# The spread G row of layers 2 and 3: ACT copies it from SBUF to PSUM, where TensorE made five transposes

## The chip, the cores and the metric

One core of a Trainium2 chip runs the whole kernel in one launch. The metric is the device time of the execution in microseconds (us); less is better. The engines are TensorE (PE; its weight loads are listed as PEld), VectorE (DVE), ScalarE (ACT), GpSimd (POOL) and SyncE (SP, which here only starts DMAs).

## The reference

A graph network with 3125 nodes of 128 features and 103125 directed edges (among them one self loop per node, to which each layer adds one more). `x = x + L0(relu(layernorm(x)))`, where L0 is two graph-attention layers with a relu between them; then `x = x + L1(relu(layernorm(x)))`, where L1 is one. Each attention layer does, for its own weights:

```python
h = x @ W
s = h @ a_src
d = h @ a_dst
e = leaky_relu(s[src] + d[dst], 0.2)
m = segment_max(e, dst)
ex = exp(e - m[dst])
out = segment_sum((ex / z[dst])[:, None] * h[src], dst)   # z = segment_sum(ex, dst)
```

The edge features are not used for the result.

## The kernel before, in words

**Dense attention over counts.** The edge list is first turned into a table C of counts (how many edges go from node i to node j, one byte each), which stays in SBUF. The three attention layers then work on dense tiles. The exponential of a leaky relu of a sum falls apart into factors of source and destination: for a source tile and a destination row it is, up to factors that are applied elsewhere, the larger of a number per source (`r_src`) and a number per destination, the G row (`g_row`), times the count.

**Chunks and tiles.** The 3125 nodes are 25 tiles (T) of 125 (P). A layer goes through its destinations in 5 chunks (NC) of 625 columns (CD, five tiles of 125), and in each chunk through the 25 source tiles s. Chunks are numbered q = 0 to 14 through all three layers (Q = 15), c = q % 5 within a layer, and a chunk that opens layer 2 or 3 (q = 5, 10) is called a turn.

**One source tile, two ways.** The weights of source tile s are max(G row, r_src) times the counts, 125 x 625, in one of nine buffers (`slot`). Most even tiles are made by VectorE in one instruction (`product`, line 1023), which reads the G row, spread over all partitions, from PSUM at column 1024 (ROWU). The tiles in `POOL_OF` (the odd ones from 3 on; in layers 2 and 3 also 6, 12 and 18, in layer 3 also 0; in the turns 20 and 22) are made by ACT and POOL: ACT takes the maximum in two instructions (`row_maximum`, lines 1428 and 1434), reading a second copy of the spread G row in SBUF (`ga`, one buffer for odd and one for even chunks), and POOL multiplies with the counts (line 662). TensorE then multiplies each finished tile with the features of its sources (`products`, line 1679; the last two tiles of a chunk in `last_products`, line 1687). A float32 matmul is two records in the trace, a transpose one.

**Where the two copies of the G row come from.** `g_row` holds the numbers with the destinations over partitions. For PSUM, TensorE spreads a column with a transpose of a broadcast, five per chunk (`fast_rows`, line 1663), at source tile `rows_at` (22, in a turn 23) of the chunk before; it waits until VectorE's last product and joined top of that chunk are done. For SBUF, SP writes `g_row` to DRAM once per layer part (`write_lines`, line 469) and loads 625 numbers, broadcast to all partitions, one chunk ahead (`ga_load`, line 478); ACT's first row maximum of a chunk waits for that load (`ga_loaded`).

**The order on each engine** is written out by hand, by chunk and source tile. Where a chunk ends:

- VectorE makes the product of tile 24, then five steps of the running maxima of the *next* chunk (`next_top`, lines 947 and 945; the steps 0 to 4 need no G row), then waits for `rows_ready` and makes the product of tile 0 (where POOL has tile 0, in chunks 11 to 14, it only waits).
- ACT makes its row maxima six source tiles ahead (`PASS_AHEAD`). At tile 24 it makes that of tile 5 of the next chunk, which waits until TensorE is through tile 21 and so has freed the buffer. Then it moves the sums of the finished chunk out of PSUM (`move_sums`, lines 1402 and 1405), at tile 0 of the next.
- TensorE, after the transposes, does the last products and those of tiles 0 and 1, then transposes the joined maxima (`top_transpose`, line 1649), which VectorE reduces (line 957). In a turn that transpose stands at the end of the chunk before.
- The middle of a chunk holds the work on the sums of the chunk before: normalisation (statistics on VectorE, scalars on POOL, line 1374 on ACT), transposes (1702) and new features (1732 or 1735) on TensorE, and moves of them on ACT (1345, 1366).

```python
dve.wait_ge(F.rows_ready, q + 1)
v.scalar_tensor_tensor(slot[s]..., tiles(ROWU), r_src[L % 2][:, s:s + 1], C5[:, c, s, :]..., ALU.max, ALU.mult)
```

Of the kernel before, what the change touches and what calls it, by code (L numbers as in the profile page):

```python
# [7 lines left out]
def gat_stack_kernel(nc, x, edges, apart, W1, a_src1, a_dst1, b1, W2, a_src2, a_dst2, b2,  # L8
# [3 lines left out]
    ALU, ACT, AX = mybir.AluOpType, mybir.ActivationFunctionType, mybir.AxisListType  # L12
# [6 lines left out]
    P = 125  # L19
    T = N // P  # L20
# [14 lines left out]
    CT = 5  # L35
# [28 lines left out]
    with ctx:  # L64
# [351 lines left out]
        def rows_at(q):  # L416
            return 23 if turn(q) else 22
# [4 lines left out]
        def prod_no(q, s):  # L422
            return q * T + s - pool_no(q, s)
# [836 lines left out]
        def _(act):  # L1260
# [151 lines left out]
            def row_maximum(q, s):  # L1412
# [16 lines left out]
                if q < NC:  # L1429
# [4 lines left out]
                a_.activation(A, A, ACT.Identity, bias=r_src[L % 2][:, s:s + 1],  # L1434
                              scale=r_src[L % 2][:, s:s + 1]).then_inc(rowmax_ok, 1)

            def scale_features(s):
                a_.activation(hB3[:, s, :], hA[:, s, :], ACT.Copy, scale=e_src[0][:, s:s + 1]).then_inc(h_scaled, 1)

            def chunk(q):  # L1440
                L, c = q // NC, q % NC
                for s in range(T):
                    if q == 0 and s + FIRST < T:
                        scale_features(s + FIRST)
                    if q:
                        if s == 0:
                            move_sums(q - 1, True)
                        if s == post_at(q).kappa:
                            factors(q - 1)
                        after_sums(F, q - 1, post_at(q), s)  # L1450
                    if c == NC - 1 and L < LAYERS - 1:
                        if s == 10:
                            act.wait_ge(sig_ready, L + 2)
                            exps_dst(L + 1, 0, EARLY_TILES)
                            exps_src(L + 1, 0, EARLY_TILES)
                        if s == T - 1:
                            act.wait_ge(F.new_sb, q)
                            exps_src(L + 1, EARLY_TILES, LATE)
                    if turn(q):
                        if s == post_at(q).act[2]:  # L1460
                            act.wait_ge(F.new_sb, q)
                            exps_src(L, LATE, T)
                        if s == 22:
                            exps_dst(L, EARLY_TILES, T)
                    for i in (q, q + 1):
                        for p in POOL_OF[i] if i < Q else ():
                            if pass_at(i, p) == q * T + s:
                                row_maximum(i, p)

            act.wait_ge(half_out[0], T + 1)  # L1470
            act.wait_ge(half_out[1], T + 1)
# [79 lines left out]
        def _(pe):  # L1551
# [100 lines left out]
            def fast_rows(q):  # L1652
                L, c = q // NC, q % NC
                if c == 0:
                    pe.wait_ge(g_done, LINES[L, 0])
                elif L and c == EARLY_TILES // CT:
                    pe.wait_ge(g_done, LINES[L, EARLY_TILES])
                if q:
                    pe.wait_ge(prod_done, prod_no(q, 0))
                for t in range(CT):  # L1660
                    if t == CT - 1 and q:
                        pe.wait_ge(F.top_done, q * (T + 1))
                    last = tr(ps[0:P, ROWU + 128 * t:ROWU + 128 * t + P],  # L1663
                              g_row[L % 2][:, c * CT + t:c * CT + t + 1].broadcast_to([P, P]), ident[0:P, 0:P])
                last.then_inc(F.rows_ready, 1)
# [83 lines left out]
            def chunk(q):  # L1749
                L, c = q // NC, q % NC  # L1750
                for s in range(T):
# [12 lines left out]
                    if q:  # L1764
# [4 lines left out]
                                pe.wait_ge(ga_ready, 1)  # L1769
                            top_transpose(F, q - 1)  # L1770
                        after_sums(F, q - 1, post_at(q), s)
                    if s == rows_at(q) and q < Q - 1:
                        fast_rows(q + 1)
                    if s == T - 1 and c == NC - 1:
                        if L < LAYERS - 1:
# [111 lines left out]
```

## Time and profile before

| what | value |
|---|---|
| runs of the kernel, median of 3 | 758.86 us (758.7 to 760.88) |
| the profiled execution, its own time | 762.35 us |
| its span, first to last instruction | 760.5 us |
| TensorE busy | 654.9 us (86%) |
| VectorE busy | 695.5 us (91%) |
| ACT busy | 506.4 us (67%) |
| POOL busy | 372.1 us (49%) |
| mean granted clock of TensorE | 0.933 of full speed |

Up to about 228 us the counts are made; then come the fifteen chunks, five per layer. The times of the trace are microseconds from the start of the span. A busy share is a mean over all stages, and an engine that is busy for nearly all of a chunk is a candidate for its bound. A number in brackets behind a timeline row is how long the engine stood before the instruction, and for whom; a row without one had no wait that the profile records. The span of an instruction can overlap the next one's by some 0.1 us, as engines are pipelined.

### The profile page before, as it was taken

The numbers are of one execution on the slowest core, as the hardware profiler recorded it, in microseconds if no ns is written. First come the engines' busy times: TensorE is split into PE (matmuls) and PEld (weight loads), VectorE is DVE, ScalarE is ACT, GpSimd is POOL, SyncE is SP. The second block draws the span as 40 slices with busy tenths as digits, with TensorE's granted clock in tenths as the row PEclk, the third lists the DMA queues.
The fourth block names the chain that finished last, engine by engine and source line by source line (L and its number), as shares of the span: only waits on it lengthen the run. The fifth ranks groups of instructions, "written<-read, shape, count | busy, mean of one in ns | idle before, by whom it ended". The sixth has DMA issues, their size and how long they took to land.

```text
span 760.5 us, 14385 instructions
## 1 busy us (share of the span) xinstructions
PE 654.9 (86%) x5581; PEld 637.2 (84%) x5581; DVE 695.5 (91%) x903; ACT 506.4 (67%) x739; POOL 372.1 (49%) x344
## 2 busy tenths in 40 slices
PE   2429999999858999999998989999979989998994
PEld 2428888889758999999998989998969888998984
DVE  3799999999959999999998899899998989999994
ACT  1205454545539987878776777878776698697880
POOL 5030000000323673645494567667587776795873
PEclk9959899899857999999999989999999999999998
DMA  3310000000003232222133232222033223323211
GB/s 81 97 43 1 1 1 2 1 1 1 1 8 59 74 104 79 82 78 74 31 74 118 72 75 100 75 82 75 27 67 95 72 66 84 108 92 118 79 55 39
DMA packets 50145, 45.39 MB, mean 60 GB/s; under 512 B 13458, under 2 KB 47995, under 8 KB 50070
## 3 DMA queue, kind: packets, MB, share of 16 engines
q1 hardware_dynamic: 49270, 43.14, 19.8%
q0 software_dynamic: 800, 1.26, 0.6%
q8 instruction: 46, 0.75, 0.4%
q14 instruction: 29, 0.24, 0.1%
HBM read 31.34 MB, written 13.05 MB: 58 GB/s over the span
## 4 chain that ended last, share of the span: by engine, by line
PE 29%; DVE 21%; issue 8%; DMA 5%; ACT 3%; POOL 3%; DVEq 0%; SPq 0%; POOLq 0%
PE ps L1679 23%; DVE ps L945 10%; DVE scratch L1023 5%; DVE ps L947 2%; DMA g_lines<-g_row 1%; DMA gathered<-ext_lines 1%; ACT scratch L1428 1%; POOL scratch L662 1%; PE ps L1687 1%; PE ps L1732 1%; DVE mu L957 1%; DMA gathered<-g_lines 1%; PE ps L1710 1%; ACT scratch L1434 1%; ACT scratch L1374 1%
## 5 line engine op out<-in xcount | busy, mean ns | idle before, releaser
L1679 PE MATMUL ps<-hB,scratch 125*125 125x129 f32 x3450 | 408.9, 277 | 29.6 <-DVE scratch L1023 22.5
L1679 PEld LDWEIGHTS ps<-hB,scratch 125*125 125x125 f32 x3450 | 394.5, 190 | 39.1 <-DVE scratch L1023 29.4
L662 POOL TENSOR_TENSOR scratch<-scratch 125x625 f32<-125x625 f32 x197 | 262.0, 1338 | 155.6 <-ACT scratch L1434 142.7
L945 DVE SCALAR_TENSOR_TENSOR ps<-C,a_unit,ps 125x625 f32<-125x625 uint8 x330 | 277.0, 863 | 2.1
L1428 ACT ACTIVATE scratch<-gathered,r_inv 125x625 f32<-125x625 f32 x197 | 159.1, 808 | 34.9 <-PE ps L1679 28.3
L1434 ACT ACTIVATE scratch<-scratch,r_src 125x625 f32<-125x625 f32 x197 | 178.4, 905 | 4.7
L1023 DVE SCALAR_TENSOR_TENSOR scratch<-ps,r_src,C 125x625 f32<-125x625 f32 x178 | 152.7, 858 | 10.8 <-PE ps L1663 10.2
L1610 PE MATMUL ps<-scratch 128*128 128x125 bf16 x1250 | 148.3, 296 | 15.5 <-DVE scratch L856 12.0
L1610 PEld LDWEIGHTS ps<-scratch 128*128 128x128 bf16 x1250 | 143.2, 121 | 19.2 <-DVE scratch L856 12.7
L1304 ACT ACTIVATE C<-ps 125x1750 uint8<-125x1750 f32 (+3 forms) x50 | 74.3, 1488 | 107.6 <-PE ps L1610 107.6
L856 DVE TENSOR_TENSOR scratch<-key_col,hB 128x6500 bf16<-128x6500 bf16 (+3 forms) x26 | 92.8, 3569 | 0.0
L856 DVE TENSOR_TENSOR scratch<-key_lo,hB 128x6656 bf16<-128x6656 bf16 (+3 forms) x26 | 88.0, 3383 | 4.2 <-PE ps L1610 4.2
L712 POOL TENSOR_TENSOR xr<-xr,b2r 125x3200 f32<-125x3200 f32 x1 | 7.3, 7338 | 151.3 <-ACT hA L1292 151.3
L1432 ACT ACTIVATE scratch<-C 125x625 bf16<-125x625 uint8 x55 | 39.3, 715 | 0.0
L1687 PE MATMUL ps<-hB,scratch 125*125 125x129 f32 x300 | 35.6, 273 | 0.0
L1687 PEld LDWEIGHTS ps<-hB,scratch 125*125 125x125 f32 x300 | 34.2, 187 | 0.1
L947 DVE TENSOR_SCALAR ps<-C,a_unit 125x625 f32<-125x625 uint8 x30 | 25.9, 863 | 3.6 <-ACT C L1304 2.6
L672 POOL TENSOR_TENSOR scratch<-scratch,rz 125x640 f32<-125x640 f32 x14 | 17.6, 1254 | 7.6 <-DVE rz L1000 7.4
L1366 ACT ACTIVATE hA<-ps 125x384 f32<-125x384 f32 (+1 forms) x20 | 8.3, 442 | 17.3 <-PE ps L1732 12.1
L1589 PE MATMUL ps<-covered,ones_f 125*125 125x1 f32 x2 | 0.6, 358 | 20.2 <-DVE covered L837 20.2
L1589 PEld LDWEIGHTS ps<-covered,ones_f 125*125 125x125 f32 x2 | 0.5, 308 | 20.5 <-DVE covered L837 20.5
L1402 ACT ACTIVATE scratch<-ps 125x387 f32<-125x387 f32 x15 | 7.3, 489 | 15.4 <-PE ps L1687 15.3
(161 smaller groups left out, 430.6 us busy)
## 6 DMA issues: line engine op xcount, KB each, us to landing
scratch<-counts_bf SPq DMA_DIRECT2D x142, 152.6 KB
counts_bf<-scratch SPq DMA_DIRECT2D x73, 152.6 KB
gathered<-g_lines SPq DMA_DIRECT2D x14, 305.2 KB
xr<-in_x SPq DMA_DIRECT2D x1, 1562.5 KB
out<-xr SPq DMA_DIRECT2D x5, 312.5 KB
edge_sb<-in_edges SPq DMA_DIRECT2D x1, 805.7 KB
gathered<-ext_lines SPq DMA_DIRECT2D x5, 122.1 KB
w<-in_W SPq DMA_DIRECT2D x2, 128.0 KB
```

Source lines behind the costliest of these rows:

```text
L662: g.tensor_tensor(slot[s], slot[s], wide[r % WIDE], ALU.mult).then_inc(pool_done, 1)
L856: last = v.tensor_tensor(hot[:, g0:g1, :, :], keys.unsqueeze(2).broadcast_to([128, g1 - g0, m, LANES]), iota_t[:, 0:m, :].unsqueeze(1).bro ...
L945: v.scalar_tensor_tensor(dest, counts, unit[:, s:s + 1], top, ALU.min, ALU.max).then_inc(S.top_done, 1)
L947: v.tensor_scalar(dest, counts, unit[:, s:s + 1], None, ALU.min).then_inc(S.top_done, 1)
L1023: v.scalar_tensor_tensor(slot[s].rearrange("p (t n) -> p t n", n=P), tiles(ROWU), r_src[L % 2][:, s:s + 1], C5[:, c, s, :].rearrange("p (t ...
L1304: a_.activation(C5[:, c, :, rows].rearrange("p t (w q) -> p t w q", q=WQ), tiles(at_, w1_ - w0).rearrange("p w (t q) -> p t w q", q=WQ), A ...
L1428: a_.activation(A, ga[q % 2], ACT.Relu, bias=-1.0, scale=r_inv[L % 2][:, s:s + 1]).then_inc(over_done, 1)
L1432: a_.activation(wide[r % WIDE], C5[:, c, s, :], ACT.Copy).then_inc(cast_act, 1)
L1434: a_.activation(A, A, ACT.Identity, bias=r_src[L % 2][:, s:s + 1], scale=r_src[L % 2][:, s:s + 1]).then_inc(rowmax_ok, 1)
L1610: last = mm(ps[0:128, o:o + WC], hot_lo[i][:, at_g, :, lane], hot_col[i][:, at_g, :, lane], start=(k == 0), stop=(k == KC - 1))
L1679: last = mm(ps[0:P, acc_at(t):acc_at(t) + HW], A[:, P * t:P * (t + 1)], feat, start=opens and t in (0, 3), stop=closes, skip_group_check=True)
L1687: last = mm(ps[0:P, acc_at(t):acc_at(t) + HW], slot[s][:, P * t:P * (t + 1)], hB3[:, s, :], start=False, stop=s == T - 1, skip_group_check ...
```

## The change

TensorE's `fast_rows` is called for chunks 0 to 4 only. For chunks 5 to 14 a new function of ACT, `copied_rows`, copies the spread G row from `ga` in SBUF to ROWU in PSUM in one ACTIVATE of 125 x 625. It stands at the end of source tile 24 of the chunk before, behind that tile's row maxima, and waits for the load of `ga`, for VectorE's last product and for the joined top. It raises the same semaphore that VectorE waits for.

```diff
--- before.py
+++ after.py
@@ -1434,6 +1434,12 @@
                 a_.activation(A, A, ACT.Identity, bias=r_src[L % 2][:, s:s + 1],
                               scale=r_src[L % 2][:, s:s + 1]).then_inc(rowmax_ok, 1)
 
+            def copied_rows(q):
+                act.wait_ge(ga_loaded, 16 * q)
+                act.wait_ge(prod_done, prod_no(q, 0))
+                act.wait_ge(F.top_done, q * (T + 1))
+                a_.activation(tiles(ROWU), ga[q % 2].rearrange("p (t n) -> p t n", n=P), ACT.Copy).then_inc(F.rows_ready, 1)
+
             def scale_features(s):
                 a_.activation(hB3[:, s, :], hA[:, s, :], ACT.Copy, scale=e_src[0][:, s:s + 1]).then_inc(h_scaled, 1)
 
@@ -1466,6 +1472,8 @@
                         for p in POOL_OF[i] if i < Q else ():
                             if pass_at(i, p) == q * T + s:
                                 row_maximum(i, p)
+                    if s == T - 1 and NC - 1 <= q < Q - 1:
+                        copied_rows(q + 1)
 
             act.wait_ge(half_out[0], T + 1)
             act.wait_ge(half_out[1], T + 1)
@@ -1653,8 +1661,6 @@
                 L, c = q // NC, q % NC
                 if c == 0:
                     pe.wait_ge(g_done, LINES[L, 0])
-                elif L and c == EARLY_TILES // CT:
-                    pe.wait_ge(g_done, LINES[L, EARLY_TILES])
                 if q:
                     pe.wait_ge(prod_done, prod_no(q, 0))
                 for t in range(CT):
@@ -1769,7 +1775,7 @@
                                 pe.wait_ge(ga_ready, 1)
                             top_transpose(F, q - 1)
                         after_sums(F, q - 1, post_at(q), s)
-                    if s == rows_at(q) and q < Q - 1:
+                    if s == rows_at(q) and q < NC - 1:
                         fast_rows(q + 1)
                     if s == T - 1 and c == NC - 1:
                         if L < LAYERS - 1:
```

`prod_no(q, 0)` is the number of products that VectorE has made when chunk q begins, and `q * (T + 1)` that of the steps and joins of the maxima.

## Rows read from the trace of the kernel before

**Rows 1.** total of the waits (who <- for whom: us, times, longest)

```profile
DVE scratch L1023 <- PE ps L1663: 10.2, 6, 2.9
```

**Rows 2.** windows, chunk 8 (length; PE, PEld, DVE, ACT, POOL busy; PEclk, DMA, GB/s)

```profile
511.64:544.94 33.30, 31.11 (x278) 30.52 (x277) 32.58 (x55) 27.65 (x42) 23.12 (x21) 1.00 0.21 64
```

**Rows 3.** timeline, boundary into chunk 8 (start, us, engine, instruction, [idle before])

```profile
511.59 0.91 ACT L1434 ACTIVATE scratch<-scratch,r_src 125x625 f32<-125x625 f32 x1
511.64 0.71 PE L1663 MATMUL ps<-ident,g_row 125*125 125x125 f32 x5
512.46 0.87 DVE L1023 SCALAR_TENSOR_TENSOR scratch<-ps,r_src,C 125x625 f32<-125x625 f32 x1
517.43 0.81 DVE L957 TENSOR_REDUCE mu<-ps 125x5 f32<-125x625 f32 x1 [0.22 <-PE ps L1649]
```

**Rows 4.** timeline, boundary into chunk 5

```profile
403.66 0.71 PE L1663 MATMUL ps<-ident,g_row 125*125 125x125 f32 x5
404.51 0.87 DVE L1023 SCALAR_TENSOR_TENSOR scratch<-ps,r_src,C 125x625 f32<-125x625 f32 x1 [1.53 <-PE ps L1663]
406.41 0.71 PE L1649 MATMUL ps<-ident,scratch 125*125 125x125 f32 x5
406.83 0.91 ACT L1434 ACTIVATE scratch<-scratch,r_src 125x625 f32<-125x625 f32 x1
413.87 4.86 PE L1679 MATMUL ps<-hB,scratch 125*125 125x129 f32 x40 [0.94 <-DVE scratch L1023]
```

**Rows 5.** groups by line, ACT, 625 columns (count; busy us, mean ns; idle before)

```profile
L1432 ACT ACTIVATE scratch<-C 125x625 bf16<-125x625 uint8 x55 | 39.3, 715 | 0.0
L1345 ACT ACTIVATE scratch<-ps 128x625 f32<-128x625 f32 x10 | 6.8, 678 | 4.1 <-PE ps L1702 4.1
L1434 ACT ACTIVATE scratch<-scratch,r_src 125x625 f32<-125x625 f32 x197 | 178.4, 905 | 4.7
```

**Rows 6.** timeline, boundaries into chunks 6, 10, 11, 12 and 13

```profile
441.33 0.91 ACT L1434 ACTIVATE scratch<-scratch,r_src 125x625 f32<-125x625 f32 x1
441.93 0.86 DVE L1023 SCALAR_TENSOR_TENSOR scratch<-ps,r_src,C 125x625 f32<-125x625 f32 x1
...
584.50 0.87 DVE L1023 SCALAR_TENSOR_TENSOR scratch<-ps,r_src,C 125x625 f32<-125x625 f32 x1 [2.88 <-PE ps L1663]
584.85 0.91 ACT L1434 ACTIVATE scratch<-scratch,r_src 125x625 f32<-125x625 f32 x1
...
620.66 0.87 DVE L947 TENSOR_SCALAR ps<-C,a_unit 125x625 f32<-125x625 uint8 x1
621.72 0.91 ACT L1434 ACTIVATE scratch<-scratch,r_src 125x625 f32<-125x625 f32 x1
622.54 0.47 ACT L1402 ACTIVATE scratch<-ps 125x387 f32<-125x387 f32 x1
...
653.16 0.91 ACT L1434 ACTIVATE scratch<-scratch,r_src 125x625 f32<-125x625 f32 x1
653.96 0.87 DVE L947 TENSOR_SCALAR ps<-C,a_unit 125x625 f32<-125x625 uint8 x1 [1.06 <-PE ps L1663]
658.99 0.81 DVE L957 TENSOR_REDUCE mu<-ps 125x5 f32<-125x625 f32 x1 [0.29 <-PE ps L1649]
...
683.52 0.91 ACT L1434 ACTIVATE scratch<-scratch,r_src 125x625 f32<-125x625 f32 x1
686.75 0.87 DVE L947 TENSOR_SCALAR ps<-C,a_unit 125x625 f32<-125x625 uint8 x1
```

**Rows 7.** windows after two long stops of TensorE

```profile
451.50:455.50 4.00, 4.00 (x18) 4.00 (x19) 3.51 (x8) 2.42 (x4) 2.21 (x2) 0.50 0.29 69
570.60:573.00 2.40, 2.39 (x12) 2.40 (x13) 2.40 (x4) 2.37 (x4) 2.40 (x3) 0.50 0.22 14
```

**Rows 8.** timeline, TensorE after the same two stops

```profile
451.50 14.21 PE L1679 MATMUL ps<-hB,scratch 125*125 125x129 f32 x100 [2.99 <-DVE scratch L1023]
...
570.61 1.30 PE L1702 MATMUL ps<-ident,scratch 125*128 125x125 f32 x5 [2.68 <-ACT scratch L1374]
```

## The prediction

> **What bounds the kernel now.** I read the total of the waits first, then the busy time of one chunk, then the instructions on both sides of each boundary between two chunks, since that is the only place the change touches. The change concerns ten boundaries, those into chunks 5 to 14.
>
> The reader is to see three things. First, VectorE seldom waits for the five transposes: six times, 10.2 us in the whole run [rows 1]. Second, inside layer 2 VectorE is the bound: from the transposes of one chunk to those of the next are 33.30 us, of which VectorE is busy for 32.58 and TensorE for 31.11 [rows 2]. Third, the boundary into chunk 8 is exactly tight [rows 3]. TensorE begins the five transposes at 511.64 and ends them at 512.35; VectorE, with the five tiles of work that it does ahead just behind it, starts the first product of the chunk at 512.46 without a recorded wait. ACT, at the same moment, is not early: its last row maximum of the chunk starts at 511.59 and lasts 0.91 us. The new copy stands behind that instruction.
>
> **The change, part by part.** *Removed:* five transposes at ten boundaries. Five of them last 0.71 us to the end of the last one [rows 3, 4], but TensorE goes on to the next instruction before that: 278 records in 31.11 us [rows 2] is 0.11 us from one to the next, so it gets back 5 x 0.11 = 0.55 us per boundary, 5.5 us in all. I put this at nothing: behind the transposes TensorE does its last products and then needs the first product of the new chunk, which VectorE makes later than now. What hides it is VectorE's lateness; were TensorE the bound, the whole 5.5 us would be a gain (a rival below). The dropped wait of TensorE on g_done costs and gives nothing, since the DMA that ACT waits for already stands behind the same exponentials.
>
> *Added on ACT:* ten copies of 125x625 float32. The trace has no ACT instruction that reads SBUF and writes PSUM at this size. The nearest row is the plain Copy of L1432, SBUF to SBUF, the same 625 columns with no scale or bias from memory: 715 ns [rows 5]. Bounds are the plain Copy out of PSUM, 678 ns, and the Identity with a scale and a bias from memory, 905 ns [rows 5]. I take 0.715, for the lack of such operands. Page "ScalarE: Activation LUTs" of the Trainium skill (the tips under "Step-by-step: what each stage is for") says that PSUM is the lower-latency destination for ACT; no row here has that direction, and if writing PSUM saved what reading it does, 0.04 us a copy, the sum below would be 0.3 us smaller.
>
> The copy starts 0.82 us after the start of the L1434 before it (the spacing to the next instruction on ACT, 621.72 to 622.54 [rows 6], a little under its 0.91 duration), ends 0.72 later, and VectorE takes some 0.04 to start: **1.58 us after the start of that L1434**. That sum is now applied to each boundary.
>
> *Waits added for ACT:* for the row's DMA, which the first row maximum of the same chunk has already waited for; for the last product and the joined top of the old chunk, which VectorE made before it went ahead. All are past. *Behind the copy on ACT* stand the moves of the sums (L1402): in layer 2's steady chunks they wait for TensorE anyway. SP's and POOL's queues get nothing and lose nothing; POOL's products wait for ACT's row maxima, which move 0.7 us where ACT is dense. The copy writes the same columns of PSUM, so nothing else is moved.
>
> *Boundary into 5* [rows 4]: ACT is held by the round trip of the row through DRAM, its last L1434 starts at 406.83, rows now come at 408.41, and VectorE, which started at 404.51, loses **3.90**. TensorE waits 0.94 for VectorE at 413.87 already, so the loss reaches it, and from there TensorE is dense to the end of the chunk.
>
> *Into 6* [rows 6]: 441.33 + 1.58 = 442.91 against 441.93: **0.98**.
>
> *Into 8* [rows 3] *and 7* (the same pattern 33.3 us earlier): 511.59 + 1.58 = 513.17 against 512.46, 0.71. Of it 0.22 vanishes, because VectorE's reduction at 517.43 waits 0.22 for TensorE's transposes of the tops, which come no later than now: the 0.55 given back pays for the later first product. **0.49** twice. *Into 9*, the same pattern 33.3 us later, but small reductions stand where that wait was: **0.71**.
>
> *Into 10* [rows 6]: 584.85 + 1.58 = 586.43 against 584.50: **1.93**.
>
> *Into 11* [rows 6]: ACT is dense, its L1434 starts at 621.72; rows come at 623.30 where VectorE went on at 620.66: 2.64 late. From there to the next boundary VectorE has no wait. *Into 12*: it would arrive at 652.90 (653.96 less its wait of 1.06), with the delay 655.54, later than the copy (653.16 + 1.58 = 654.74), and 1.58 later than the 653.96 of now; the reduction at 658.99 had waited 0.29. Together **1.29** for both boundaries.
>
> *Into 13* [rows 6] *and 14* (the same pattern): copy ready at 683.52 + 1.58 = 685.10, VectorE wants it at 686.75: **0**, with 1.6 us to spare; here the first tile belongs to POOL, so VectorE needs the row later.
>
> Sum of delays: 3.90 + 0.98 + 0.49 + 0.49 + 0.71 + 1.93 + 1.29 = **9.8 us**. By the ends of the copy's price (678 and 905 ns) over seven binding boundaries it is 9.5 to 11.1.
>
> *TensorE's clock.* Where TensorE stood for 2.99 us (before 451.50) or 2.68 us (before 570.61) the granted clock was 0.50 afterwards, the 1.2 GHz level; after 0.94 us (413.87) the work ran at full speed [rows 4, 7, 8]. At half clock 18 records took 4.00 us in one window and 12 took 2.40 in the other; at 0.11 each they need 2.0 and 1.3, so such a fall costs at least 1.1 us and, as the first lasted longer than its window, up to 3.0 (100 records in 14.21 us [rows 8], 11.2 at that pace). Into chunk 5 TensorE will have finished the tops' transposes at about 406.5 and wait for the first product, done 0.87 after 408.41, at 409.28: a stop of 2.8 us, between the two that brought a fall, and more short stops follow it (the third product comes 3.9 late too). Part of the slow stretch lies under those stops. I take **1.5 us** for it, bounds 0 and 3.0, paid in full because TensorE is dense afterwards.
>
> Total 9.8 + 1.5 = **11.3 us**. The profiled execution took 762.35 us with a span of 760.5, so 1.85 lie around the span; it would become 773.7. The median of the runs is 758.86, 3.5 under the profiled one; the difference is carried over: **770.2 us**.
>
> **The rivals.**
>
> *A. The clock keeps full speed at chunk 5.* For: the stop is worked out to a few tenths of a microsecond, and the rows leave open what a stop between 0.94 and 2.68 us does; if the copy or the products come a little sooner it is such a one. Then 758.9 + 9.8 = 768.7.
>
> *B. More falls of the clock.* In chunk 11 TensorE waits for the moved sums, which start 0.72 after the 622.54 of now [rows 6] while TensorE is there 0.55 sooner, and again for products that VectorE makes 2.64 late. With 3.0 at chunk 5 and 1.5 here: 758.9 + 9.8 + 4.5 = 773.2. Against: in chunk 11 TensorE later waits for POOL, which would swallow most of it.
>
> *C. The delays are absorbed.* VectorE's lateness in the steady chunks may be taken up by TensorE's 0.55 and by the shared slack, so that only the boundaries where ACT is held by a DMA (5 and 10) count: 3.9 + 1.9 = 5.8, 764.7. If those are eaten too, 761. Against: VectorE is busy 32.58 of 33.30 us and has nowhere to catch up.
>
> *D. Faster: TensorE is the bound.* Place: the products behind the removed transposes. If each 0.55 us is on the path, the kernel takes 758.9 - 5.5 = 753.4. It decides from the point where ACT's copy is done before TensorE would have been: ACT's last L1434 would have to start some 0.8 us earlier than it does [rows 3]. For: TensorE is busy 31.11 us of the 33.30 [rows 2]. Against: ACT is late at every boundary up to 12 [rows 3, 4, 6].
>
> *E. The change does not relieve TensorE in profile terms* (transposes still there): not possible for chunks 5 to 14, as the call is taken out; no chance is given.
>
> **How the numbers follow.** Forecast (with one fall of the clock, and sizes within a microsecond or two) 0.50; A 0.24; B 0.08; C 0.12, of which 0.05 ends within 0.3%; D 0.05; the rest, 0.01, anything. A difference of 0.3% (2.3 us) is about what a measurement of this kernel can tell from none. Faster 0.05; same 0.06; slower 0.89. The range goes from C's 764.7 to B's 773.2, widened a little on each side for the copy's price: 764.3 to 774.0; outside are D, the end of C and the far side of B, together under 2 in 10.
>
> **What would show each step.** VectorE's wait for the row is then for the ACT copy: about 6 us or less into chunk 5 (1.53 now plus 3.9), under 1 us into chunk 8, over 2 us into 11, none into 13. The copy lasts 0.68 to 0.80 us. The stretch from the boundary into 8 to that into 9 grows from 33.30 to some 34 us; that from 13 to 14 stays as it is. The granted clock reads 0.5 for a few microseconds near 410 to 420. TensorE's idle time for VectorE's products grows by more than 5 us. The prediction is wrong if ACT's last row maximum comes earlier because TensorE ran ahead, if the copy takes over 1 us, or if layers 2 and 3 as a whole grow by less than 5 us.

## The result, and the profile after

| | before | after |
|---|---|---|
| median of 4 runs each | 759.36 us (758.7 to 760.88) | 772.26 us (769.86 to 774.13) |
| ratio | | 1.0165, 95% interval 1.0132 to 1.0199 |
| profiled execution, its span | 762.35, 760.5 | 769.86, 768.0 |
| TensorE, VectorE, ACT busy | 654.9, 695.5, 506.4 | 652.3, 695.8, 512.0 |
| mean granted clock | 0.933 | 0.933 |

The kernel became slower by 1.65%, 12.9 us between the medians. The predicted 770.2 us lies 2.1 us under the measured median, which is inside the range of 764.3 to 774.0. The two profiled executions differ by 7.5 us only, because that of before is slower than all four runs and that of after the fastest of its four; so times are compared by the runs, and the traces are used for places.

Lines behind the new function have moved down by six to eight in the kernel after: L1663 is L1669 there, L1679 is L1685, L1649 is L1657 and L1687 is L1693. `copied_rows` is L1441.

The total of the waits (who waited for whom: us in total, times, longest), first one row of the kernel before, then three of the kernel after, of which the first answers to [rows 1]:

```profile
PE ps L1679 <- DVE scratch L1023: 22.5, 25, 3.0
...
DVE scratch L1023 <- ACT ps L1441: 14.4, 6, 5.8
DVE ps L947 <- ACT ps L1441: 2.5, 1, 2.5
PE ps L1685 <- DVE scratch L1023: 35.3, 38, 3.0
```

VectorE waits for ACT's copy in seven of the ten places, for 16.9 us. In the kernel before it waited for the transposes into the same ten chunks four times, for 7.7 us: 1.53, 2.27 and 2.88 for the product and 1.06 for L947 [rows 3, 4, 6]. The 10.2 us of [rows 1] leave the last one out and hold 3.5 us of layer 1, which the change does not touch. VectorE's busy time did not change. TensorE had less to do and stood 12.8 us longer for VectorE's products.

The copy itself, by its line (duration in ns, least, median, most):

```profile
L1441 ACT ACTIVATE ps<-gathered x10: 672/673/675, 407.4 to 723.8; 125x625 f32<-125x625 f32 x10
```

Timeline of the kernel after at the boundary into chunk 9, the steady pattern, which answers to [rows 3]: ACT, then VectorE.

```profile
513.23 0.91 ACT L1434 ACTIVATE scratch<-scratch,r_src 125x625 f32<-125x625 f32 x1
514.04 0.67 ACT L1441 ACTIVATE ps<-gathered 125x625 f32<-125x625 f32 x1
514.82 0.87 DVE L1023 SCALAR_TENSOR_TENSOR scratch<-ps,r_src,C 125x625 f32<-125x625 f32 x1 [0.68 <-ACT ps L1441]
```

This boundary is put beside the boundary into 8 of before, since the pattern repeats. The copy starts 0.81 us after the start of the L1434 and VectorE 0.11 after the copy's end: 1.59 us after the start of the L1434, where the prediction had 1.58. The wait of 0.68 answers to the predicted 0.71.

Timelines of the kernel after, VectorE's first instruction that needs the row, into chunks 5, 6, 10, 11 and 13, which answer to [rows 4, 6]:

```profile
408.21 0.87 DVE L1023 SCALAR_TENSOR_TENSOR scratch<-ps,r_src,C 125x625 f32<-125x625 f32 x1 [5.63 <-ACT ps L1441]
...
445.50 0.87 DVE L1023 SCALAR_TENSOR_TENSOR scratch<-ps,r_src,C 125x625 f32<-125x625 f32 x1 [0.90 <-ACT ps L1441]
...
591.60 0.87 DVE L1023 SCALAR_TENSOR_TENSOR scratch<-ps,r_src,C 125x625 f32<-125x625 f32 x1 [5.80 <-ACT ps L1441]
...
630.35 0.87 DVE L947 TENSOR_SCALAR ps<-C,a_unit 125x625 f32<-125x625 uint8 x1 [2.50 <-ACT ps L1441]
...
694.34 0.86 DVE L947 TENSOR_SCALAR ps<-C,a_unit 125x625 f32<-125x625 uint8 x1
```

The reader sees the two turns with over 5 us each, 2.5 us into chunk 11, and nothing into 13.

**Where the time came from, chunk by chunk.** VectorE joins its two running maxima once per chunk (L951). The table gives the time from one join to the next, read from the timelines of VectorE; the column "into q" holds the boundary into chunk q, and below "the stretch into q" is that time. The stretch of 33.30 us in [rows 2], which goes from the boundary into 8 to that into 9, has most of its length in the same chunk as the column "into 8". Two profiles were had of each kernel; the second ones are explained under the experiments.

```
us from join to join   into 5  into 6  into 7  into 8  into 9  into 10  into 11  into 12  into 13  into 14
before, first           39.04   34.86   35.63   33.29   35.82    39.14    32.13    33.96    31.87    32.06
before, second          38.61   34.89   34.33   33.30   34.97    38.94    31.84    34.26    31.89    32.07
after, first            42.02   35.12   34.42   34.42   37.24    42.06    34.32    32.26    31.88    32.07
after, second           42.23   35.12   34.41   34.43   36.99    41.68    35.24    32.06    31.88    32.05
```

By the means of each pair the growth is 3.3 (into 5), 0.2, -0.6, 1.1, 1.7, 2.8, 2.8, -2.0 and nothing for the last two: 9.5 us in these four traces. The runs say 12 to 13. Both profiled executions of the kernel before (762.35 and 760.39 us) were slower than the medians beside them (759.36 and 759.83), so some 3 us of the loss have no place in this table.

### The profile page after: what moved, and what is told of

The parts are those of the page before. It is cut to its first block, busy times and chain, and to the rows that moved or that the text cites. A ratio compares the mean times of both kernels' runs of the same rounds, so it can differ in the third digit from the quotient of the medians.

```text
span 768.0 us, 14301 instructions
## 1 busy us (share of the span) xinstructions
PE 652.3 (85%) x5531; PEld 632.9 (82%) x5531; DVE 695.8 (91%) x903; ACT 512.0 (67%) x749; POOL 372.1 (48%) x344
## 4 chain that ended last, share of the span: by engine, by line
PE 27%; DVE 25%; issue 8%; ACT 4%; DMA 4%; POOL 1%; DVEq 0%; SPq 0%; ACTq 0%; POOLq 0%
PE ps L1685 22%; DVE ps L945 12%; DVE scratch L1023 6%; DVE ps L947 2%; ACT scratch L1428 2%; DMA g_lines<-g_row 1%; DVE mu L957 1%; PE ps L1738 1%; ACT scratch L1374 1%; DMA gathered<-g_lines 1%; PE ps L1716 1%; DVE m_top L963 1%; ACT scratch L1434 1%; DMA gathered<-ext_lines 1%; PE ps L1741 1%
## 5 line engine op out<-in xcount | busy, mean ns | idle before, releaser
L1685 PE MATMUL ps<-hB,scratch 125*125 125x129 f32 x3450 | 411.1, 278 | 40.9 <-DVE scratch L1023 35.3
L1685 PEld LDWEIGHTS ps<-hB,scratch 125*125 125x125 f32 x3450 | 395.5, 190 | 52.2 <-DVE scratch L1023 46.1
L662 POOL TENSOR_TENSOR scratch<-scratch 125x625 f32<-125x625 f32 x197 | 261.9, 1338 | 157.4 <-ACT scratch L1434 144.3
L1434 ACT ACTIVATE scratch<-scratch,r_src 125x625 f32<-125x625 f32 x197 | 178.4, 905 | 4.7
L1618 PEld LDWEIGHTS ps<-scratch 128*128 128x128 bf16 x1250 | 143.1, 121 | 18.8 <-DVE scratch L856 12.5
L1693 PE MATMUL ps<-hB,scratch 125*125 125x129 f32 x300 | 35.8, 274 | 0.4 <-POOL scratch L662 0.4
L1693 PEld LDWEIGHTS ps<-hB,scratch 125*125 125x125 f32 x300 | 34.2, 187 | 0.8 <-POOL scratch L662 0.8
L947 DVE TENSOR_SCALAR ps<-C,a_unit 125x625 f32<-125x625 uint8 x30 | 25.9, 863 | 5.1 <-ACT C L1304 2.6
L1410 ACT ACTIVATE kappa<-back 125x5 f32<-125x5 f32 x15 | 3.1, 207 | 31.8 <-DVE back L970 31.8
```

Of the source, the lines that this page charges most:

```text
L662: g.tensor_tensor(slot[s], slot[s], wide[r % WIDE], ALU.mult).then_inc(pool_done, 1)
L947: v.tensor_scalar(dest, counts, unit[:, s:s + 1], None, ALU.min).then_inc(S.top_done, 1)
L1618: last = mm(ps[0:128, o:o + WC], hot_lo[i][:, at_g, :, lane], hot_col[i][:, at_g, :, lane], start=(k == 0), stop=(k == KC - 1))
L1685: last = mm(ps[0:P, acc_at(t):acc_at(t) + HW], A[:, P * t:P * (t + 1)], feat, start=opens and t in (0, 3), stop=closes, skip_group_check=True)
L1693: last = mm(ps[0:P, acc_at(t):acc_at(t) + HW], slot[s][:, P * t:P * (t + 1)], hB3[:, s, :], start=False, stop=s == T - 1, skip_group_check ...
```

## The experiments

The theory to be tested: what costs is that the row reaches VectorE late, by the copy's place behind ACT's last row maximum. The rivals: ACT's added work wherever it stands; TensorE's time; the copy's use of PSUM.

**The kernel before again.** No edit.

> The kernel before, unchanged, for a second profile. In the first profile of it TensorE's clock fell in chunk 6 (behind the 2.99 us stop), and that execution was 3.5 us above the median. If such falls are what makes executions of one kernel differ, this profile has another count of falls and its time differs by 1 to 3 us for each; if they always come at the same place, the timeline of the first is repeated to 0.2 us. Ratio 1.000 +- 0.003.

Measured: 759.83 us, ratio 0.9987 (0.9971 to 1.0004). The profile repeats the first but for a few places (the table above), the widest of them into 7, 1.3 us shorter. TensorE's clock fell in chunk 6 in both, behind stops of 2.99 and 3.00 us, but not for equally long: 100 records took 14.21 us in the first [rows 8] and 12.94 in the second, 1.27 less. So this fall repeats in its place and not in its length, which the expectation had not allowed for. A stretch of layer 2 can differ by 1 us between executions of the same kernel.

**The kernel after again.** No edit.

> The changed kernel again, for its size over more executions and a second profile. 769 to 774 us, ratio to before 1.0125 to 1.018. In the steady chunks of layer 2 the stretch between boundaries is again 34.4 us (33.3 before): 0.7 wait for the copy and 0.7 in VectorE's two small operations L960 and L963, which end where a POOL product ends, less 0.2.

Measured: 770.42 us, ratio 1.0165 (1.0147 to 1.0184), over kernels run beside it 12 us. The steady stretch is 34.42 again.

**What the removal alone is worth.**

```diff
-                for t in range(CT):
+                for t in (range(CT) if q < NC else (CT - 1,)):
```

> The kernel before with one of the five transposes for each of chunks 5 to 14 (the rows of the other four tiles stay those of chunk 4): what the removal alone is worth, 4 x 0.11 x 10 = 4.4 us of TensorE. My theory (VectorE bounds the steady chunks): what it gains is only where VectorE waited for the transposes (into 7, 10 and 12), 0.44 us each, so 0 to 1.5 us, ratio 0.998 to 1.000. Rival (TensorE is the bound): 4 to 5 us less, ratio 0.994.

Measured: 760.77 us against 760.27, ratio 0.9998 (0.9983 to 1.0013). The 4.4 us less on TensorE (by the estimate above) bought nothing in total, and the rival of a TensorE bound, which wanted 4 to 5 us, falls. But the nothing is a sum. From join to join, against the means of the two profiles of before, the stretches into 5, 6 and 7 became shorter by 0.7, 0.4 and 1.1 us (38.11, 34.44, 33.91), and those into 8 and 9 longer by 1.2 and 1.3 (34.51, 36.74). The total of the waits does not show it; TensorE's for VectorE's products grew by 0.9 us only:

```profile
DVE scratch L1023 <- PE ps L1663: 8.8, 7, 2.7
PE ps L1679 <- DVE scratch L1023: 23.4, 24, 2.9
```

What made the two stretches longer is read below, beside the late transposes.

**The copy one place earlier, and two.** From the changed kernel, the call is moved ahead of the row maxima, at source tile 24 or at 22:

```diff
+                    if s == T - 1 and NC - 1 <= q < Q - 1:     # or T - 3
+                        copied_rows(q + 1)
                     for i in (q, q + 1):
...
-                    if s == T - 1 and NC - 1 <= q < Q - 1:
-                        copied_rows(q + 1)
```

> The changed kernel with ACT's copy one place earlier: ahead of the row maximum of tile 5, at the start of source tile 24. Theory (what costs is the place of the copy behind ACT's last row maximum): VectorE's wait for the copy goes to nothing in the steady chunks of layer 2, the row comes before the 512.46 of the kernel before also where TensorE was late (into 7 and 9/10), into 11 the copy is ready at once; the ten or so us are gone, 755 to 760 us, ratio to before 0.995 to 1.002. Rival 1 (ACT's added 6.7 us of work is what costs, wherever it stands): no better than the changed kernel, 768 to 773. Rival 2 (the delay is from writing PSUM while VectorE reads it): also 768 to 773, with VectorE's instructions longer.

> The changed kernel with ACT's copy ahead of the row maximum of source tile 22, two places earlier than the run before this one. Theory: ACT stands idle 1.9 us there in layer 2 and waits for VectorE's last product at most 0.3 us; the row is there 2 to 4 us before VectorE wants it at every boundary; only at boundary 5 and 10 does it hang on the DMA, coming 0.7 us after it. 754 to 758 us, ratio 0.993 to 0.999, below the kernel before, since its 2.27 and 2.88 us waits for TensorE into 7 and 10 are gone as well. Rival (ACT now stands behind VectorE's last product and its row maxima come late): over 760.

Measured: 765.09 us at tile 24, ratio 1.0055 (1.0032 to 1.0078), and 761.48 us at tile 22, ratio 1.0011 (0.9990 to 1.0031). With the same copies, ten of 0.67 to 0.70 us, the loss goes from 1.65% to 0.55% and to nothing that can be told. The theory stands in its main point: the place decides, not ACT's added work and not the use of PSUM. Both were expected lower. At tile 24 VectorE still waits 3.96 us for the copy into 5 and 0.84 into 11. At tile 22 VectorE no longer waits for the row in chunk 8:

```profile
508.28 0.70 ACT L1441 ACTIVATE ps<-gathered 125x625 f32<-125x625 f32 x1
510.10 0.82 ACT L1428 ACTIVATE scratch<-gathered,r_inv 125x625 f32<-125x625 f32 x1 [1.13 <-PE ps L1685]
```

```profile
512.52 0.87 DVE L1023 SCALAR_TENSOR_TENSOR scratch<-ps,r_src,C 125x625 f32<-125x625 f32 x1
518.38 0.81 DVE L957 TENSOR_REDUCE mu<-ps 125x5 f32<-125x625 f32 x1 [1.12 <-PE ps L1657]
```

The first fence is ACT, the second VectorE. The copy lies in ACT's idle time, VectorE goes on without a wait, and then waits 1.12 us for TensorE's transposes of the tops, where it had waited 0.22. The trace shows where that comes from, one chunk earlier:

```profile
483.66 1.20 DVE L960 SCALAR_TENSOR_TENSOR e_top<-mu,b_low 125x5 f32<-125x5 f32 x1
485.56 0.96 DVE L963 SCALAR_TENSOR_TENSOR m_top<-e_top 125x5 f32<-125x5 f32 x1
...
487.57 12.94 PE L1685 MATMUL ps<-hB,scratch 125*125 125x129 f32 x100 [2.84 <-DVE scratch L1023]
```

Two small operations of VectorE (0.17 and 0.52 us in chunk 7 of the kernel before) are long in chunk 7, TensorE stands 2.84 us for VectorE's product where it had stood 1.18, and the clock granted to it over the next 4 us is 0.65, so that 100 records take 12.94 us and not 11.54. With that TensorE is late for chunk 8. The stop into 7 that was to vanish (2.27 us) is gone, and such losses stand in its place.

**Which boundaries.** From the changed kernel, ACT copies only into the chunks named and TensorE makes the others, with the wait for the later exponentials put back:

```diff
-                    if s == T - 1 and NC - 1 <= q < Q - 1:
+                    if s == T - 1 and q + 1 in (5, 10):     # (6, 7, 8, 9), (11, 12, 13, 14)
...
-                    if s == rows_at(q) and q < NC - 1:
+                    if s == rows_at(q) and q < Q - 1 and q + 1 not in (5, 10):
```

> ACT copies into chunks 5 and 10 only, TensorE makes the transposes everywhere else, as before. By the sum: 3.9 + 1.9 = 5.8 us over the kernel before, ratio 1.0076 (1.005 to 1.010); by the first trace of the changed kernel a little more, 4.1 + 3.6, 1.010. Rival (delays at one boundary are taken up later): under 1.004.

> ACT copies into chunks 6, 7, 8 and 9 only. By the sum 1.0 + 0.5 + 0.5 + 0.7 = 2.7 us, ratio 1.0035. By the traces after (1.1 per chunk, since POOL now also holds up VectorE's small operations there): 4.3 us, ratio 1.0057, and the row of L963 at 0.96 us instead of 0.52.

> ACT copies into chunks 11 to 14 only. By the sum 1.3 us over the kernel before, all from the boundaries into 11 and 12, ratio 1.0017 (1.000 to 1.004); into 13 and 14 the timeline is that of before. Rival (each copy costs its 0.7 us on ACT): 2.8 us, 1.0037.

Measured, with the kernel before at 758.48 us: the turns 1.0079 (1.0054 to 1.0104), 6.0 us; chunks 6 to 9 1.0076 (1.0049 to 1.0102), 5.8 us; chunks 11 to 14 1.0036 (1.0017 to 1.0055), 2.7 us. These microseconds are the ratio times 758.48; between the medians they are 5.0, 5.2 and 2.5. Together 14.5, where all ten at once cost 12.5 in the same batch by the ratio (12.8 and 11.9 between the medians): the 1 to 2 us between are shared or within the intervals. The turns are as summed (5.8). Chunks 6 to 9 cost twice the 2.7 of the sum (3.7 to 7.7 by the interval) and some more than the 4.3 of the trace. Layer 3 cost 2.7 for 1.3, which is the low end of its interval (1.3 to 4.2); in its own trace the stretches into 11 and 12 are 35.29 and 32.07, together 1.3 over both profiles of before. The stretches into 7 and 8 of the middle run are 34.42 and 34.41 us again, so that part is made in these chunks and not inherited from the turn.

**Late without a copy.** The kernel before, TensorE repeating six transposes into chunks 6 to 9:

```diff
-                for t in range(CT):
+                for t in (range(CT) if q < NC + 1 or q > 2 * NC - 1 else (0, 1, 2, 3, 0, 1, 2, 0, 1, 2, CT - 1)):
```

> No copy on ACT at all: the kernel before, but TensorE repeats six of the transposes into chunks 6, 7, 8 and 9, so the row is ready 0.66 us later (about 513.0 where it was 512.35, as late as ACT's copy makes it). Theory (lateness of the row costs, and it is more than the lateness itself, because it shifts VectorE's small operations L960 and L963 into POOL's products): the stretch between the boundaries into 8 and 9 is 34.2 to 34.5 us instead of 33.30, as with ACT's copy, L963 there lasts 0.8 to 1.0 us; 4 to 7 us more in all, as in the run with ACT's copy at 6 to 9 (ratio 1.0076). Rival (ACT's copy itself, its use of PSUM or its place ahead of the moved sums): the stretch is 33.3 + 0.5 to 0.7 and the whole 1.5 to 3 us.

Measured: 760.94 us, ratio 1.0033 (1.0019 to 1.0048), 2.5 us. VectorE's wait is 0.61 us, almost that of the copy, yet from the boundary into 8 to that into 9 it was 33.97 us (34.42 with the copy): 33.30 and the lateness. My version of the theory fell here, and the rival's sizes were right. Why can be read from where POOL's products stand. Three fences, each with VectorE's first product of the chunk (that of the kernel before stands in [rows 3]), then VectorE's two small operations and POOL's products around them.

The kernel after (chunk 7):

```profile
480.40 0.87 DVE L1023 SCALAR_TENSOR_TENSOR scratch<-ps,r_src,C 125x625 f32<-125x625 f32 x1 [0.69 <-ACT ps L1441]
485.97 0.42 DVE L960 SCALAR_TENSOR_TENSOR e_top<-mu,b_low 125x5 f32<-125x5 f32 x1
487.09 0.96 DVE L963 SCALAR_TENSOR_TENSOR m_top<-e_top 125x5 f32<-125x5 f32 x1
...
483.43 1.38 POOL L662 TENSOR_TENSOR scratch<-scratch 125x625 f32<-125x625 f32 x1 [2.19 <-ACT scratch L1434]
485.08 1.29 POOL L662 TENSOR_TENSOR scratch<-scratch 125x625 f32<-125x625 f32 x1 [0.27 <-ACT scratch L1434]
486.74 1.29 POOL L662 TENSOR_TENSOR scratch<-scratch 125x625 f32<-125x625 f32 x1 [0.37 <-ACT scratch L1434]
```

The kernel before (chunk 8):

```profile
518.35 0.17 DVE L960 SCALAR_TENSOR_TENSOR e_top<-mu,b_low 125x5 f32<-125x5 f32 x1
519.21 0.52 DVE L963 SCALAR_TENSOR_TENSOR m_top<-e_top 125x5 f32<-125x5 f32 x1
...
516.76 1.37 POOL L662 TENSOR_TENSOR scratch<-scratch 125x625 f32<-125x625 f32 x1 [2.73 <-ACT scratch L1434]
518.41 1.29 POOL L662 TENSOR_TENSOR scratch<-scratch 125x625 f32<-125x625 f32 x1 [0.28 <-ACT scratch L1434]
```

The late transposes (chunk 8):

```profile
512.18 0.87 DVE L1023 SCALAR_TENSOR_TENSOR scratch<-ps,r_src,C 125x625 f32<-125x625 f32 x1 [0.61 <-PE ps L1663]
518.07 0.17 DVE L960 SCALAR_TENSOR_TENSOR e_top<-mu,b_low 125x5 f32<-125x5 f32 x1
518.93 0.52 DVE L963 SCALAR_TENSOR_TENSOR m_top<-e_top 125x5 f32<-125x5 f32 x1
...
516.49 1.38 POOL L662 TENSOR_TENSOR scratch<-scratch 125x625 f32<-125x625 f32 x1 [3.39 <-ACT scratch L1434]
518.14 1.29 POOL L662 TENSOR_TENSOR scratch<-scratch 125x625 f32<-125x625 f32 x1 [0.27 <-ACT scratch L1434]
```

From VectorE's first product to POOL's first product behind it, it is 4.30 us in the kernel before (516.76 less the 512.46 of [rows 3]), 4.31 with the late transposes, and 3.03 with the copy. Late transposes hold back TensorE's last products too, and with them the moved sums, ACT's row maxima and POOL; the whole pattern moves. With the copy only VectorE is late (0.7), while TensorE is early (0.55 by the prediction's estimate), so POOL comes 1.27 us sooner for VectorE, and the two small operations fall into its products. L960 then ends at 486.39 and POOL's product at 485.08 + 1.29 = 486.37; L963 ends at 488.05 and the next product at 488.03. They last 0.25 and 0.44 us longer than before.

The run with the removal alone tells the two apart. It has no copy and no late row, only an earlier TensorE, and in its chunk 8 POOL's first product stands 3.91 us behind VectorE's (513.12 less 509.21). VectorE, then POOL, then TensorE behind them:

```profile
514.78 1.30 DVE L960 SCALAR_TENSOR_TENSOR e_top<-mu,b_low 125x5 f32<-125x5 f32 x1
516.77 0.96 DVE L963 SCALAR_TENSOR_TENSOR m_top<-e_top 125x5 f32<-125x5 f32 x1
...
514.77 1.29 POOL L662 TENSOR_TENSOR scratch<-scratch 125x625 f32<-125x625 f32 x1 [0.27 <-ACT scratch L1434]
516.42 1.29 POOL L662 TENSOR_TENSOR scratch<-scratch 125x625 f32<-125x625 f32 x1 [0.36 <-ACT scratch L1434]
...
518.78 12.86 PE L1679 MATMUL ps<-hB,scratch 125*125 125x129 f32 x100 [2.83 <-DVE scratch L1023]
```

Both operations end 0.02 us behind a product of POOL's. (In its chunks 7 and 9, where VectorE did wait for the one transpose, POOL's product stands 4.31 us behind and L960 lasts 0.17, as before.) TensorE then stands 2.83 us instead of 1.18 and its granted clock is 0.59 over the next 4 us. So what costs more than the lateness is not the copy: it comes with the transposes that were taken away, whose time brings POOL forward.

**Moving one of the two, in both kernels.** L963 goes from source tile 3 to source tile 2 in the chunks of layer 2 behind the turn, right behind L960.

```diff
-At(1, (2, 2, 3, 3), 4, (4, 4, 4), (9, 9), ...
+At(1, (2, 2, 2, 3), 4, (4, 4, 4), (9, 9), ...
```

> The changed kernel with VectorE's m_top (L963) moved from source tile 3 to 2 in the chunks of layer 2, right behind e_top (L960). In the changed kernel L960 ends where one POOL product ends (486.39 against 486.37) and L963 where the next one ends (488.05 against 488.03). Theory (a small VectorE operation that reads and writes SBUF is held until POOL's product is through): one hold remains for the two, L963 lasts 0.16 us, and the stretch between the boundaries into 8 and 9 falls from 34.42 to 33.8 to 34.0; 1 to 2 us less in all. Rival (L963 is long by itself or by its semaphore): L963 stays at 0.5 us or more and the stretch at 34.4.

> The same move of L963 in the kernel before. There L960 slips into the gap between two POOL products (518.35 to 518.52, products until 518.13 and from 518.41), and L963 placed right behind it would start inside the next product and be held until 519.70. Theory: L963 lasts 1.0 to 1.2 us where it lasted 0.52, and the stretch grows from 33.30 to 33.6 to 34.0, so the same move helps the one kernel and harms the other. Rival: no change, or a gain as in the changed kernel.

Measured: in the changed kernel 769.72 us, ratio 1.0143 (1.0120 to 1.0166), which can't be told from the 1.0165 without the move; in the kernel before 764.38 us, ratio 1.0074 (1.0051 to 1.0097), a clear loss of 5.9 us. Timeline of the changed kernel with the move, VectorE and then POOL:

```profile
520.13 0.42 DVE L960 SCALAR_TENSOR_TENSOR e_top<-mu,b_low 125x5 f32<-125x5 f32 x1
520.59 0.17 DVE L963 SCALAR_TENSOR_TENSOR m_top<-e_top 125x5 f32<-125x5 f32 x1
521.45 0.76 DVE L970 SCALAR_TENSOR_TENSOR back<-m_top,back_of 125x5 f32<-125x5 f32 x1
...
519.25 1.29 POOL L662 TENSOR_TENSOR scratch<-scratch 125x625 f32<-125x625 f32 x1 [0.27 <-ACT scratch L1434]
520.90 1.29 POOL L662 TENSOR_TENSOR scratch<-scratch 125x625 f32<-125x625 f32 x1 [0.36 <-ACT scratch L1434]
```

And of the kernel before with it:

```profile
519.01 0.17 DVE L960 SCALAR_TENSOR_TENSOR e_top<-mu,b_low 125x5 f32<-125x5 f32 x1
519.21 1.17 DVE L963 SCALAR_TENSOR_TENSOR m_top<-e_top 125x5 f32<-125x5 f32 x1
...
519.07 1.29 POOL L662 TENSOR_TENSOR scratch<-scratch 125x625 f32<-125x625 f32 x1 [0.27 <-ACT scratch L1434]
```

L963 lasts 0.17 in the one, as expected, and 1.17 in the other, to within 0.02 us of the end of POOL's product (519.07 + 1.29 = 520.36). In the changed kernel the hold passed to the next small operation, L970, now 0.76 us, and the stretch into 8 fell only from 34.42 to 34.20. (That into 7 is 35.25 there, since the clock fell in chunk 6.) In the kernel before the loss is larger than the 0.65 us of the hold per chunk: the stretch into 8 is 36.14 us, 2.8 over before. The trace shows the rest. L970 is held too (below), and VectorE had waited 1.35 us for the transposes into 8, at 513.12:

```profile
521.08 0.96 DVE L970 SCALAR_TENSOR_TENSOR back<-m_top,back_of 125x5 f32<-125x5 f32 x1
```

0.65 + 0.79 + 1.35 = 2.79. The transposes are late because the same holds in chunk 7 made TensorE stand 2.62 us, behind which 100 records took 12.94 us. In chunk 8 it stood 2.61 us and the 100 records took 11.54: the clock did not fall.

**The copy twice.** The changed kernel, a second copy behind the first:

```diff
-    a_.activation(tiles(ROWU), ..., ACT.Copy).then_inc(F.rows_ready, 1)
+    a_.activation(tiles(ROWU), ..., ACT.Copy).then_inc(careful_b2, 1)
+    act.wait_ge(careful_b2, q - NC + 1)
+    a_.activation(tiles(ROWU), ..., ACT.Copy).then_inc(F.rows_ready, 1)
```

> The changed kernel with the copy made twice, the second behind the first, at all ten boundaries: a dose of 0.8 us more of lateness. By the sum: 0.8 at the boundaries into 5 to 10 and about 0.8 once for 11 and 12, none into 13 and 14, 5 to 6 us over the changed kernel, ratio to before 1.023 to 1.025. Rival (each microsecond on ACT counts anywhere): 8 us, 1.027. Where the clock of TensorE falls behind a longer stop it can be more.

Measured: 773.57 us, ratio 1.0194 (1.0174 to 1.0215), so some 3 us over the changed kernel (770.42; 2.2 by the ratios) where 5 to 6 were expected. In the steady chunks of layer 2 the waits doubled as they should; at the turns they hardly grew (6.19 for 5.63 into 5, 5.50 for 5.80 into 10). Timeline into chunk 9, VectorE:

```profile
516.12 0.87 DVE L1023 SCALAR_TENSOR_TENSOR scratch<-ps,r_src,C 125x625 f32<-125x625 f32 x1 [1.40 <-ACT ps L1443]
521.70 0.17 DVE L960 SCALAR_TENSOR_TENSOR e_top<-mu,b_low 125x5 f32<-125x5 f32 x1
522.55 0.66 DVE L963 SCALAR_TENSOR_TENSOR m_top<-e_top 125x5 f32<-125x5 f32 x1
```

The wait is 1.40 instead of 0.68, but the holds went from 0.42 and 0.96 back to 0.17 and 0.66, 0.55 less, so the chunk grew by 0.17 only (34.59 against 34.42). Lateness and time are not in proportion, since each shift also changes what meets POOL.

## Why the prediction was right

**The mechanism** was the one named: the copy stands behind ACT's last row maximum, and VectorE gets the row later. Moving the copy takes the loss away and the removal of the transposes alone gives nothing in total. The direction and the total held, the total in part by luck, as the terms below show; 11.3 us were summed and 12.9 (12.0 in the second comparison) measured.

**The price of the copy** was 0.715 us, measured 0.673. It lies 5 ns under the lower bound that was taken from the read of PSUM, 0.678. The Trainium skill's tip on PSUM as the nearer destination ("ScalarE: Activation LUTs", the tips under "Step-by-step: what each stage is for") agrees, by 0.042 us against the plain Copy to SBUF of [rows 5], though those two also differ in their types. VectorE's start took 0.11, not 0.04, and so the 1.58 us held by two errors that cancel. No row had the 0.04; [rows 3] has 0.11 between the end of the transposes and VectorE's start.

**The delays by boundary.** Turn 5: 3.9 predicted, 3.3 in the traces. Turn 10: 1.9, 2.8 in the traces; the two turns alone 5.8 and 6.0, and in the trace of that run 3.7 and 2.0. Into 6: 0.98 predicted and a wait of 0.90 for the copy, but the stretch grew by 0.2 only. There the holds went the other way: L960 lasts 1.11 us in chunk 5 and 0.92 in chunk 6 of the kernel before (0.47 and 0.92 in the second profile) and 0.17 in both after. Into 11 and 12 together 1.3, against 0.8 in the traces (2.8 less 2.0) and 2.7 (1.3 to 4.2 by the interval; 1.3 in its trace) when run alone; that the delay into 11 is partly given back at 12 was seen rightly. Into 13 and 14 zero, and zero. Into 6 to 9 the sum 2.7 was too small: 5.8 when run alone.

**The term that was mis-sized** is that of the boundaries 7 to 9, "0.49 twice" and 0.71. The steady stretch grew by 1.12. The step that failed is "I put this at nothing" of the 0.55 us given back to TensorE, for which VectorE's lateness was the only reason. The wait was right (0.68 for 0.71) and so was the 0.22 that vanishes; left out was that VectorE's small operations are held by POOL's products, and that the 0.55 us given back to TensorE brings POOL forward against VectorE. 0.68 + 0.25 + 0.44 - 0.22 = 1.15, where 1.12 was measured. In chunk 9 the same hold fell on L874, which lasts 1.34 us (552.33 in the trace after) and 0.17 before.

**The clock term** of 1.5 us failed in its size. The clock did fall in chunk 5. Timeline of TensorE after the stop, and the window behind it (length; PE, PEld, DVE, ACT and POOL busy; granted clock; DMA; GB/s):

```profile
409.14 6.59 PE L1685 MATMUL ps<-hB,scratch 125*125 125x129 f32 x40 [2.96 <-DVE scratch L1023]
416.44 4.86 PE L1685 MATMUL ps<-hB,scratch 125*125 125x129 f32 x40 [0.72 <-DVE scratch L1023]
```

```profile
409.14:412.50 3.36, 3.36 (x17) 3.36 (x18) 3.25 (x6) 1.24 (x2) 1.52 (x2) 0.55 0.35 121
```

The stop of 2.96 us (2.8 predicted) was followed by a clock of 0.55 of full speed, near the 1.2 GHz level, and 40 records took 6.59 us, where 40 at full speed take 4.67. But behind them TensorE still waited 0.72 us for VectorE, so the 1.9 us were hidden. The run of the changed kernel with L963 moved is the same up to there, its TensorE stood 2.79 us and its clock did not fall: from VectorE's first product to the start of the 90 records that TensorE later runs in one piece are 24.53 us there (407.14 to 431.67) and 24.54 here (408.21 to 432.75). In the second profile of the kernel after, the clock was at 0.50 from 412.5 to 416.5 and the same stretch is 25.25 us (407.69 to 432.94). So the fall cost nothing in one profile and 0.7 us in the other. I had named the cover ("part lies under those stops") and then charged for it in full.

In exchange, both profiles of the kernel after lack a fall that both of before have in chunk 6. There the stop before source tile 4 was 3.0 us [rows 8], and after the change it is 2.24:

```profile
454.33 6.87 PE L1685 MATMUL ps<-hB,scratch 125*125 125x129 f32 x60 [2.24 <-DVE scratch L1023]
462.11 4.67 PE L1685 MATMUL ps<-hB,scratch 125*125 125x129 f32 x40 [0.91 <-DVE scratch L1023]
```

100 records are 11.5 us here, 14.21 and 12.94 in the two profiles of before. The stretch into 7 is 34.42 and 34.41 us after, as the steady one, while before it is 1.0 and 2.3 us over the steady 33.30. That the clock makes such a difference is seen in the changed kernel with L963 moved, where the clock did fall in chunk 6, behind a stop of 2.22 us, and the stretch into 7 is 35.25. The length of the stop does not tell by itself whether the clock falls: it did after 2.22 us there and not after 2.24 here, nor after 2.78 in chunk 6 with the copy at tile 22. What decides stays open.

So the terms for the clock and for the boundaries into 5 and 6 were too high, those for the stretches into 8, 9 and 10 too low, and the fall that went away in chunk 6 was in no term. That the total came out is owed to these in part.

**The rivals.** D (TensorE as the bound) is refuted in its total by the removal alone, 0.9998. C (absorbed) is refuted by the run at chunks 6 to 9. A's number, 768.7, is below all eight runs of the changed kernel, though its cost of the clock at chunk 5 (nothing) was nearer than the forecast's. B's second fall came: in chunk 11, after a stop of 2.24 us for the moved sums, 20 records took 4.10 us where they take 2.37 at full speed. The stretches into 11 and 12 grew by 0.8 us together, so the traces do not show the 1.5 that B charged for it. By the totals B and the forecast can't be told apart: the first median, 772.3, lies nearer to B's 773.2, the second, 770.4, nearer to the forecast.

**No version beat the kernel before.** The nearest is the copy at source tile 22, 1.0011 (0.9990 to 1.0031): the same time with 50 records less on TensorE. Its trace has the holds and the fall of the clock shown above.

## What to carry to other kernels

When work moves from one engine's queue to another's, price it by where the new instruction stands: read what runs just ahead of it on its new engine and when the reader wants the result; here the same ten copies cost 1.65%, 0.55% or nothing by their place. Read the receiving boundary for each stage, since slack at one of them (1.6 us in layer 3) says nothing of the others. And an engine made faster shifts the phase of what follows it: look which short operations share a resource with a long one, and whether they now fall together.

## What the runs showed of the hardware

Several small VectorE operations whose tensors all lie in SBUF are held while POOL's product (L662) runs and end 0.01 to 0.03 us after it, in every kernel here. L960, L963 and L970 (SCALAR_TENSOR_TENSOR, 125 x 5) last 0.17 us where they meet none, and 0.42 and 0.96 us (after), 0.52 (before), 1.30 and 0.96 (the removal alone), 0.42 and 0.76, and 1.17 (the moved ones) where they do. L874 (TENSOR_SCALAR, 125 x 15) lasted 1.34 us for 0.17. Not every small operation is held. In the changed kernel with L963 moved, a reciprocal (L993, 0.19 us from 641.74) and a reduction (L898, 0.41 us from 450.29) kept their usual length beside POOL's products from 641.60 to 642.89 and from 450.21 to 451.53. VectorE's large operations with PSUM as source or destination, which last 0.86 us, also run beside the same POOL products at their usual length.

An ACT copy of 125 x 625 float32 from SBUF to PSUM takes 673 ns (672 to 675 in the ten of the kernel after); moved to source tile 22 the same ten take 669 to 696.

The granted clock of TensorE fell behind some stops and not behind others of the same length: 2.62 us and 2.61 in two neighbouring chunks of one run, 2.22 and 2.24 in the same chunk of two kernels.
